# Holding each scatter of records for the last but one, and reordering the first steps and the tail of the attention stage

## What is computed

```python
h = _ln(x, ln_w, ln_b)
q, k, v = h @ Wq, h @ Wk, h @ Wv                       # 16 heads, 4 keys, 8 values each
gk = log_sigmoid(h @ gk_w1 @ gk_w2 + gk_b2) / 16
S[t] = exp(gk[t]) * S[t-1] + k[t] (x) v[t];  o[t] = q[t] . S[t]
o = _rms(o, rms_w) * silu(h @ Wg)
x1 = x + o @ Wo
x1 = x1 + gelu(_ln(x1) @ W1 + b1) @ W2 + b2
x2 = _layernorm(x + x1)                                # plain layer norm
scores = softmax(x2 @ gate_w + gate_b)                 # 8 experts, the top two are kept
for i in range(8):                                     # a later expert overwrites an earlier
    y = relu(x2 * w_i @ w1[i] + b1[i]) @ w2[i] + b2[i]
    out = where(w_i > 0, y, out)
result = _layernorm(x2 + out)
```

## Time and profile before

| | |
|---|---|
| time, median of 3 runs | 527.89 us (522.45 to 528.21) |
| profiled execution, its own time | 526.84 us |
| its span, first to last instruction | 525.0 us |
| mean granted TensorE clock | 0.903 of full speed |
| busy of the span: PE, DVE, ACT, POOL | 436.3, 364.3, 343.6, 347.0 us |
| moved by DMA | 62.42 MB, mean 119 GB/s |

### The profile page before, as it was taken

One profiled execution on the slowest core, in us unless ns is written; L12 is line 12 of the kernel. 1 busy time (PEld: TensorE's weight loads), 2 busy tenths in 40 slices (PEclk: granted clock), 3 DMA queues, 4 the chain that ended last, 5 costly groups with the idle time before them and its releaser, 6 DMA issues.

```text
span 525.0 us, 11079 instructions
## 1 busy us (share of the span) xinstructions
PE 436.3 (83%) x2755; PEld 348.4 (66%) x2755; DVE 364.3 (69%) x1205; ACT 343.6 (65%) x981; POOL 347.0 (66%) x393
## 2 busy tenths in 40 slices
PE   5769999999999948999986496520699999999994
PEld 3336766667666635778764474510699999999994
DVE  4187989989998856648673265663277777777775
ACT  2448788888887855797863284520377777777773
POOL 0037799899999895632565517563277878787785
PEclk9769999999999969999987768755599999999998
DMA  5655666555665330600111101112787767777730
GB/s 147 163 118 132 155 156 140 124 135 128 155 153 135 102 100 0 201 1 2 42 43 41 41 7 56 36 41 66 201 229 198 197 193 202 198 192 197 199 110 22
DMA packets 44668, 62.42 MB, mean 119 GB/s; under 512 B 6702, under 2 KB 30129, under 8 KB 42560
## 3 DMA queue, kind: packets, MB, share of 16 engines
q1 hardware_dynamic: 40000, 52.92, 39.4%
q0 software_dynamic: 4320, 8.47, 4.7%
q10 hardware_dynamic: 288, 0.34, 0.2%
HBM read 48.45 MB, written 13.71 MB: 118 GB/s over the span
## 4 chain that ended last, share of the span: by engine, by line
PE 42%; issue 33%; DMA 10%; SPq 6%; DVE 5%; ACT 3%; POOL 1%; ACTq 0%; DVEq 0%; POOLq 0%
PE bank L694 13%; PE bank L710 13%; DMA x_sb<-in_x 6%; PE bank L976 5%; PE bank L1001 3%; DMA values_by_head<-row_buffers 3%; PE bank L942 2%; SPq L858 2%; PE bank L701 2%; DVE states L1515 2%; SPq L871 1%; PE bank L989 1%; SPq L891 1%; DVE kv L1506 1%; PE bank L930 1%
## 5 line engine op out<-in xcount | busy, mean ns | idle before, releaser
L573 POOL DMA_INDIRECT expert_regions<-row_buffers,row_i x64 | 62.8, 982 | 58.5 <-DVE row_i L559 38.0
L840 POOL DMA_INDIRECT out_rows<-x_sb x71 | 71.0, 999 | 34.2 <-issue 26.1
L710 PE MATMUL bank<-ew,x_sb 128*128 x568 | 79.8, 284 | 0.1
L1674 POOL TENSOR_TENSOR states<-states,queries 128x1024 f32<-128x1024 f32 x32 | 75.0, 2367 | 6.5 <-DVE states L1515 6.5
L694 PE MATMUL bank<-x_sb,slab 128*128 128x128 f32 x568 | 78.3, 282 | 1.0 <-DMA slab<-in_slabs 0.6
L1515 DVE TENSOR_TENSOR_SCAN states<-bank,kv 128x512 f32<-128x512 f32 x64 | 72.9, 1200 | 1.3 <-issue 1.2
L694 PEld LDWEIGHTS bank<-x_sb,slab 128*128 128x128 f32 x568 | 70.8, 196 | 3.0 <-issue 1.0
L710 PEld LDWEIGHTS bank<-ew,x_sb 128*128 128x128 f32 x568 | 69.8, 193 | 2.3 <-issue 0.3
L976 PE MATMUL bank<-states,con 128*128 128x256 f32 x256 | 60.5, 381 | 1.5 <-DVE row_buffers L1529 1.5
L942 PE MATMUL bank<-ht,wc 128*64 128x256 f32 x320 | 47.8, 433 | 10.5 <-issue 6.7
L794 DVE TENSOR_SCALAR x_sb<-bank,slab 128x128 f32<-128x128 f32 x142 | 42.8, 343 | 16.7 <-PE bank L694 16.7
(11 more groups left out here) (188 smaller groups left out, 924.9 us busy)
## 6 DMA issues: line engine op xcount, KB each, us to landing
slab<-in_slabs SPq DMA_DIRECT2D x71, 258.0 KB
kv<-values_by_head SPq DMA_DIRECT2D x32, 512.0 KB, 6.5
x_sb<-expert_regions SPq DMA_DIRECT2D x71, 65.0 KB
x_sb<-in_x SPq DMA_DIRECT2D x32, 128.0 KB, 6.1
values_by_head<-row_buffers SPq DMA_DIRECT2D x16, 256.0 KB, 2.1
out_rows<-x_sb POOLq DMA_INDIRECT x71
expert_regions<-row_buffers,row_i POOLq DMA_INDIRECT x64
expert_regions<-pad_record SPq DMA_DIRECT2D x9, 65.0 KB, 5.3
```

The source lines that it names most:

```text
L573: pool.indirect_dma_start(out=regions, out_offset=bass.IndirectOffsetOnAxis(ap=row_i[:, q, g:g + 1].bitcast(U32), axis=0), in_=rec[:, ring ...
L710: ins = pe.matmul(bank[6 + s][:, 0:D], c_ht[:, s, c * P:(c + 1) * P], ew2[:, bass.ds(e * HC + c * D, D)], start=(c == 0), stop=(c == HC - 1))
L840: pool.indirect_dma_start(out=out, out_offset=bass.IndirectOffsetOnAxis(ap=c_id[:, q:q + 1].bitcast(U32), axis=0), in_=c_y[:, q, :], in_of ...
L1674: pool.tensor_tensor(half, half, queries[:, s, :].unsqueeze(1).to_broadcast([P, VL, T]), ALU.mult).then_inc(q_applied, 1)
```

## The change

What it does, part by part:

- GpSimd waited ahead of a batch's scatters 3, 6 and 9 for the landing of the one two before; it now does so ahead of every scatter from the third of the batch on. The last batch, with four scatters on one semaphore, has no such wait before or after.
- In the expert stage seven waits of each slot go, where another wait of the same engine already covers the same fact: three on TensorE, three on ScalarE, one on VectorE.
- In the attention loop `fold_ffn` comes at step 1 instead of 2; `rstd_first` of steps 1 and 2 comes ahead of `decay_of` and `gate_sum`; `var_first` of step 2 comes right behind `stats_first`. In every step ScalarE does `z_log_of`, `squares`, `evacuate_q` instead of `evacuate_q`, `z_log_of`, `squares`, and VectorE's `log_sigmoid` waits for `evacuate_q` of its pair as well.
- The written lists of the tail are in another order on TensorE, ScalarE, VectorE and GpSimd; `LATE_T2` moves with them. The calls are the same ones, and there are as many table loads on ScalarE.

```diff
@@ -270,7 +270,7 @@
         BATCHES = ((0, 2), (2, 5), (5, 8), (8, 11), (11, 13), (13, 15), (15, 16))
 
 
-        LATE_T2 = {14: 3, 15: 7}
+        LATE_T2 = {14: 4, 15: 10}
 
         def pair_of_banks(i):
 
@@ -568,7 +568,7 @@
                 for g in range(tiles(q)):
                     if g % 4 == 0:
                         pool.wait_ge(ln3_norm, 4 * BATCHES[q][0] + g + 4)
-                    if g and g % 3 == 0 and TURNS[q] > 1:
+                    if g >= TURNS[q] > 1:
                         pool.wait_ge(scattered[q][g % 2], 16 * (g // 2))
                     pool.indirect_dma_start(
                         out=regions,
@@ -687,8 +687,6 @@
 
                     pe.wait_ge(slab_ld[q], 16 * ((k - 3) // SLOTS_C + 1))
                     pe.wait_ge(xwt_evac, item + 1)
-                    wait_items(pe, relu_act, item, 2)
-                    wait_items(pe, relu_dve, item, 2)
 
                     for c in range(HC):
                         ins = pe.matmul(bank[2 + 2 * (c // 2) + s][:, (c % 2) * P:(c % 2 + 1) * P],
@@ -697,7 +695,6 @@
                 if live(2):
                     item, s = k - 2, (k - 2) % 2
                     pe.wait_ge(xw_done, item + 1)
-                    wait_items(pe, xwt_evac, item, 2)
                     pe.transpose(bank[s][:, 0:P], c_xw[:, s, :], ident).then_inc(xwt_done, 1)
                 if live(4):
                     item, s = k - 4, (k - 4) % 2
@@ -721,7 +718,6 @@
                 if live(2):
                     item, s = k - 2, (k - 2) % 2
                     act.wait_ge(xwt_done, item + 1)
-                    wait_items(act, h_done, item, 2)
                     act.activation(c_xwt[:, s, :], bank[s][:, 0:P], ACT.Copy).then_inc(xwt_evac, 1)
                 if live(3):
                     item, s, q = k - 3, (k - 3) % 2, (k - 3) % SLOTS_C
@@ -742,7 +738,6 @@
                 if live(1):
                     item, s, q = k - 1, (k - 1) % 2, (k - 1) % SLOTS_C
                     act.wait_ge(rc_ld[q], 16 * ((k - 1) // SLOTS_C + 1))
-                    wait_items(act, xwt_done, item, 2)
                     act.activation(c_xw[:, s, :], rc[:, q, 0:D], ACT.Copy, scale=rc[:, q, D:D + 1]).then_inc(xw_done, 1)
 
             for k in range(SLOTS + STAGES_C - 1):
@@ -789,7 +784,6 @@
                 if live(3):
                     item, s, q = k - 3, (k - 3) % 2, (k - 3) % SLOTS_C
                     dve.wait_ge(h_done, item + 1)
-                    wait_items(dve, y2_done, item, 2)
                     for c in range(2, HC):
                         ins = dve.tensor_scalar(c_ht[:, s, c * P:(c + 1) * P], bank[4 + s][:, (c - 2) * P:(c - 1) * P],
                                                 slab[:, q, H + c:H + c + 1], 0.0, ALU.add, ALU.max)
@@ -1020,7 +1014,7 @@
                 def on(s):
                     return k >= s
 
-                if k == 2:
+                if k == 1:
                     fold_ffn()
@@ -1044,94 +1038,94 @@
                     output_product(k - 3)
 
 
+            sum_keys(13, 0)
+            transpose_second(11)
+            sum_keys(13, 1)
             project_k(15)
-            sum_keys(13, 0)
-            sum_keys(13, 1)
-            transpose_second(11)
             sum_squares(13)
             first_product(0)
+            transpose_second(12)
+            first_product(1)
             sum_keys(14, 0)
             output_product(13)
-            transpose_second(12)
             sum_keys(14, 1)
-            first_product(1)
+            second_product(0)
             sum_squares(14)
-            second_product(0)
             first_product(2)
+            transpose_second(13)
             second_product(1)
             sum_keys(15, 0)
-            transpose_second(13)
             sum_keys(15, 1)
+            output_product(14)
+            sum_squares(15)
             first_product(3)
-            sum_squares(15)
-            output_product(14)
             second_product(2)
...
             logits(12)
+            second_product(14)
             transpose_rows(13)
-            second_product(14)
+            first_product(15)
+            transpose_rows(14)
             logits(13)
-            first_product(15)
+            logits(14)
             prefix(4)
-            transpose_rows(14)
-            logits(14)
             second_product(15)
-            prefix(5)
             transpose_rows(15)
             logits(15)
+            prefix(5)
             prefix(6)
 
             phase_c_pe(pe)
@@ -1265,11 +1259,11 @@
                     return k >= s
 
                 if on(2):
-                    evacuate_q(k - 2)
-                if on(2):
                     z_log_of(k - 2)
                 if on(4):
                     squares(k - 4)
+                if on(2):
+                    evacuate_q(k - 2)
                 if on(1):
                     evacuate_ht(k - 1)
                 if on(4):
@@ -1278,6 +1272,8 @@
                     sig_exp_of(k - 2)
                 if on(1):
                     evacuate_v(k - 1)
+                if k in (1, 2):
+                    rstd_first(k)
                 if on(2):
                     decay_of(k - 2)
                 if on(5):
@@ -1288,7 +1284,7 @@
                     z_abs_of(k - 1)
                 if on(5):
                     norm_second(k - 5)
-                if on(0):
+                if k not in (1, 2):
                     rstd_first(k)
                 if on(2):
                     sig_log_of(k - 2)
@@ -1300,41 +1296,41 @@
                     sig_of(k - 2)
 
 
+            z_log_of(14)
             evacuate_q(14)
-            z_log_of(14)
             squares(12)
             evacuate_ht(15)
+            sig_exp_of(14)
             rstd_heads(12)
-            rstd_second(11)
             evacuate_v(15)
             decay_of(14)
+            rstd_second(11)
+            norm_second(11)
             z_abs_of(15)
             z_exp_of(15)
-            evacuate_q(15)
             z_log_of(15)
-            sig_exp_of(14)
             sig_log_of(14)
             sig_of(14)
-            norm_second(11)
+            evacuate_q(15)
+            evacuate_h2t(11)
+            gate_sum(15)
+            decay_of(15)
             squares(13)
-            evacuate_h2t(11)
-            sig_exp_of(15)
+            rstd_second(12)
+            norm_second(12)
             rstd_heads(13)
-            decay_of(15)
-            rstd_second(12)
-            sig_log_of(15)
-            gate_sum(15)
-            sig_of(15)
-            norm_second(12)
             act.preload_act_table_set("gelu_and_others")
             gelu(0)
             evacuate_h2t(12)
-            squares(14)
             gelu(1)
             act.preload_act_table_set("natural_log_exp_and_others")
+            sig_exp_of(15)
+            sig_log_of(15)
+            sig_of(15)
+            squares(14)
             rstd_second(13)
+            norm_second(13)
             rstd_heads(14)
-            norm_second(13)
             act.preload_act_table_set("gelu_and_others")
             gelu(2)
             evacuate_h2t(13)
...
@@ -1519,6 +1515,8 @@
             def log_sigmoid(i):
 
                 dve.wait_ge(z_logged, i + 1)
+
+                dve.wait_ge(q_sb, i + 1)
                 need(dve, decay_ready, i)
                 dve.scalar_tensor_tensor(z_log[:, :], bank[2][:, 0:T], bz_neg[:, :], z_abs[:, :], ALU.min,
                                          ALU.subtract).then_inc(z_sum, 1)
@@ -1542,6 +1540,8 @@
 
                 if on(0):
                     stats_first(k)
+                if k == 2:
+                    var_first(k)
                 if on(5):
                     norm_heads(k - 5)
                 if on(3):
@@ -1554,7 +1554,7 @@
                     log_sigmoid(k - 2)
                 if on(5):
                     stats_second(k - 5)
-                if on(0):
+                if k != 2:
                     var_first(k)
                 if k == 0:
                     copy_projections()
@@ -1577,12 +1577,12 @@
             norm_heads(12)
             scan(14)
             residual(12)
+            log_sigmoid(15)
             stats_second(12)
+            var_second(12)
             outer_product(15)
-            log_sigmoid(15)
-            var_second(12)
+            scan(15)
             norm_heads(13)
-            scan(15)
             residual(13)
             stats_second(13)
             var_second(13)
...
             stats_of(13)
             logits_of(4)
             shift_of(4)
+            rows_of(14)
             choice_of(4)
-            rows_of(14)
             places_of(4)
             stats_of(14)
             logits_of(5)
             shift_of(5)
+            rows_of(15)
             choice_of(5)
-            rows_of(15)
             places_of(5)
             stats_of(15)
             logits_of(6)
@@ -1717,18 +1717,18 @@
             apply_q(13, 0)
             apply_q(13, 1)
             sum_x(11)
-            gate_of(14)
             apply_q(14, 0)
```

(36 more changed lines are left out.)

81 lines of the change are left out of this document (34 added, 47 removed).

## The result

| | before | after |
|---|---|---|
| time, median | 525.96 us (522.45 to 528.21, 4 runs) | 509.13 us (507.76 to 513.15, 4 runs) |
| ratio | | 0.972, interval 0.967 to 0.977 |
| profiled execution, its span | 525.0 us | 506.7 us |
| mean granted TensorE clock | 0.903 | 0.920 |
| busy: PE, DVE, ACT, POOL | 436.3, 364.3, 343.6, 347.0 us | 424.5, 365.1, 346.6, 347.0 us |

The account below looks back on a forecast made before the run. It took the attention loop as bound by four nearly full engines, the record stage by waits, the expert stage by TensorE; 526.84 - 4.4 (first steps) - 5.6 (tail) = 516.8, rounded to 517 us, range 505 to 528.

Parts of the forecast that it names:

- the forecast proper: Whole kernel: the predicted outcome without any rival, 511 to 522 us, chance 0.50.
- First steps, 4.4 us: Start of the attention loop: with the fold earlier, `outer_product(0)` waits for pair 3's x and starts 4.4 us earlier.
- Tail, 5.6 us: Attention tail: `project_g(15)` no longer stalls, the replicated v of pair 15 is late next, `first_product(0)` starts 5.6 us earlier.
- the lead is lost in the record stage: Record stage: its chain or new order takes back half of the 10 us or more; 522 to 530 us, chance 0.22.
- Removed waits, 0 us: Expert stage: waits are decoded while matmuls are queued, so removing them gives 0 us, at most 7.8 us over 71 slots.
- a TensorE limited by its sequencer: Expert stage, rival: the removed waits give most of 7.8 us, for 510 us; chance 0.05.
- Padding unchanged, 13.3 us: End of the record stage: the padding blocks' 13.3 us, first block to last landing, don't change.
- Holds, 0 us: Record stage scatters: 48 waits instead of 15 cost 0, since two under way is what the pace of issue gives anyway.
- the holds free TensorE: Record stage, rival: bounding a backlog of scatters dissolves the late signals, gaining 12 us, for 505 us; chance 0.12.
- the holds set the pace: Scatters of batches 1 to 4, rival: landings above 2.54 us make holds slow the kernel, 532 to 546 us; chance 0.07.

Follow-up runs that it names:

- chip A: The chip of the result table, where the kernel before took 525.96 us and the changed kernel 509.13 us, ratio 0.972.
- chip C: Two chips taken as one kind in the follow-up runs; kernel before 495.37 and 495.32 us, changed kernel 491.85 and 491.48 us, ratios 0.997 and 0.995.
- chip B: The chip of the follow-up runs with one part of the change at a time; the kernel before took 520.26 us there.

## Why the prediction was right, and where it was not

The total was right in kind and some 8 us too slow: 509 for 517. That is inside the range of 505 to 528, but below the 511 to 522 of the forecast proper, where only the rivals stood. It also took chip A: on chip C the same two kernels differ by 3.5 and 3.8 us, where the forecast has 10. Terms put at nothing, the record stage with its holds, the padding and the expert stage, gave 3.2 + 1.9 + 2.6 = 7.7 us on A by the profiles, so that the number came this close is in part luck. By its steps:

- **First steps, 4.4 us: right in size**, 3.8 measured; x was late next, by the forecast to 0.6 us. What made the fold late was in the main the stretch at a granted clock of 0.50, which the prediction left out: at 1.00 the old order gave `outer_product(0)` at 26.43. Alone the part gave 2.35 us of time on chip B by the medians (interval from 2.9 gained to 0.4 lost), so the forecast's 4.4 isn't shown in the time; where the rest went is open.
- **Tail, 5.6 us: right in size**, 5.4 to 7.3 alone on chip B and 10.6 with the first steps on A (10.0 forecast). The clock returned to 1.00, v was late next. `scan(15)` came at 193.25 instead of 207.06, 13.8 us earlier with the first steps in it, for 8.8 + 4.4 = 13.2. That it reaches the end, "the first product starts the record stage, so I take its 5.6", holds on chip C: with the old hold the changed kernel is 10.1 and 10.3 us faster than before, the forecast's 10.0 us to a few tenths. That is luck in part: the removed waits are in it, 1.3 to 1.7 us, and the list moves. It does not hold on chip B, where the tail alone gave nothing. The rival "the lead is lost in the record stage" is what happened there.
- **Removed waits, 0 us: too low by 1.7.** From the third slot's first product to the 67th slot's, the period is 2.008 to 2.014 us in the seven traces with the waits and 1.980 to 1.993 in the seven without (means 2.011 and 1.987); 0.024 us by 71 slots are 1.7 us. On chip B, where the removal is the only edit, it is 1.990 against 2.009 to 2.014, and between before and after on A 0.021, 1.5 us. The three of 1.980 all have the new hold too and are from chip C; why isn't known. The removal alone measured 0.3 us by the medians and 1.2 by the ratio, with zero in its interval. The rival of a TensorE limited by its sequencer is out; a fifth of its 7.8 us is there.
- **Padding unchanged, 13.3 us: wrong**, 11.4 (340.42 to 351.83). The prediction gave no reason for leaving it as it was. Its eight writes take 8.0 to 8.2 us in all traces from chip C and with the new hold alone on B, though scatters run beside them in some of these too; on A and B they take 9.7 to 11.9 us otherwise. What slows them there I didn't find.
- **Holds, 0 us: the step that failed.** The sentence was "where such a wait was, it mostly ended at once", with the conclusion that the pace of issue gives two under way anyway. The landings do come in time, as the earlier trace rows shows, but the price isn't there alone: a second wait in front of an issue costs 0.5 us by itself, and I had counted waits as free if their condition was met. On chip C the new hold costs 5.5 to 6.6 us, 4.3 of them by the second waits. And on B the same edit gained 6.6 us, with a padding that starts some 5 us earlier and runs 3.5 us shorter than with the waits removed alone. That is half the price of the rival "the holds free TensorE" without its mechanism: bounding the scatters helped, the late signals stayed. How it helps isn't shown. The rival "the holds set the pace" had the mechanism of chip C, and its price far too high, because a landing mostly comes 2.3 us from the start of its issue, 2.54 us to the next one.

For chip A the parts were not run, so how its 17 us split is worked out, not measured: 10.6 us of lead, 1.5 us of slots and, if the hold gains there about what it gains on B, some 6 us make 18, as found. That B's tail kernel lost its whole lead while A's changed kernel kept it speaks for the two acting together (a lead is worth something on such a chip if the hold keeps the stage in order), but no run of tail and hold together was made on B, and this stays open; so does what the list moves do by themselves. So does why the signals are late at all: the earlier trace rows suggested running scatters, yet scatters run as densely on chip C, where no signal is late, and with one under way or none held there was nothing there to cure. The two kernels that could tell, one scatter under way and no hold, did not meet a chip that stalls.

The version that beats both kernels on chip C is the changed one with the old hold, 485.0 us (0.980); without the second waits it is 487.2. On A and B neither was measured.

## What to carry to other kernels

Price a wait in front of an issue by what it does to the engine's own issue pace, not by whether its condition is met: a second wait was 0.5 us here wherever the landing was in time. When the pace of issue and the landing are of equal length (2 x 1.27 and 2.54 us), a limit of two under way has no slack and its sign hangs on what else is late. Run a change of 1 or 2% on more than one chip: the earlier start holds in every trace (`first_product(0)` at 192.6 to 196.2 with both parts, 200.7 to 204.8 with neither), but a stage full of cross-engine waits can swallow it or not. And where a wait is long, look at the granted clock of what it waits for: most of the first steps' gain was that.

## What the runs showed of the hardware

- The same kernel took 526, 520 and 495 us on the chips that it met. The attention stage differs little between them (`first_product(0)` at 202.9 to 204.8 in five traces with the old order, 200.7 in a sixth); the difference is in the record stage, where on two of the chips VectorE waits up to 11.4 us at a time (12.7 in the trace of the removed waits) for signals that the trace calls "remote", and the padding takes up to 11.9 us instead of 8.1.
- A scatter of 128 records is issued every 1.27 us; it lands 2.3 us from the start of its issue in the median (4.2 at most, with one under way), and from one issue to the next that waits for its landing is 2.54 us.
- A scatter with two waits starts 1.8 us after the last one, with one wait or none 1.27 us, where the landing is in time.
- The same first steps took until 26.43 us at a granted clock of 1.00 (from 22 to 26 us) and until 28.97 to 30.37 us at 0.50 to 0.61.
